# Output projection of the scan: the weights first in the DMA queue, the bias added to x on POOL instead of on PE

## What is computed

```
out = jnp.swapaxes(ys, 0, 1)
out = out * jax.nn.silu(gate)
out = jnp.einsum('bld,ed->ble', out, w_out) + b_out
if ts > 1:
    out = jnp.repeat(out, ts, axis=1)[:, :L]
...
x = _layernorm(x + _L0_attn_ref(...), axis=-1)
```

## Time and profile before

| | before |
|---|---|
| time, median of 3 runs | 3907.22 us (3903.13 to 3920.8) |
| time of the profiled execution | 3888.8 us |
| its span in the trace | 3887.2 us |
| mean granted TensorE clock | 0.91 |
| PE busy | 3273.1 us, 84% of the span |
| DVE busy | 2940.3 us, 76% |
| ACT busy | 2034.9 us, 52% |
| POOL busy | 1158.9 us, 30% |

### The profile page before, as it was taken

How to read it: one execution, slowest core, us unless ns; L and a number is a source line. 1 busy time by engine, 2 the same in 40 slices (tenths; PEclk the granted TensorE clock), 3 DMA queues, 4 the chain that set the end, 5 groups by cost and what they waited for, 6 DMA issues and landing times. The chain is left out here.

```text
span 3887.2 us, 70295 instructions
## 1 busy us (share of the span) xinstructions
PE 3273.1 (84%) x25130; PEld 2242.6 (58%) x25130; DVE 2940.3 (76%) x5069; ACT 2034.9 (52%) x4097; POOL 1158.9 (30%) x1404
## 2 busy tenths in 40 slices
PE   4677777771799957799999999999999955999997
PEld 1677677741688856444444444444444434888886
DVE  7999999841333447588898888988899325888888
ACT  3444444410354433256778878888888832333333
POOL 5888888605311244100111111212111120000000
PEclk7788888875899978688999999999999977999999
DMA  3000000023222126420303031220200000000001
GB/s 137 1 1 0 0 0 0 0 79 123 90 86 86 65 92 191 90 38 8 46 13 46 13 46 27 37 39 21 45 15 13 12 20 13 11 10 12 12 12 44
DMA packets 85787, 155.14 MB, mean 40 GB/s; under 512 B 16688, under 2 KB 53445, under 8 KB 83570
## 3 DMA queue, kind: packets, MB, share of 16 engines
q1 hardware_dynamic: 65202, 108.32, 11.4%
q0 software_dynamic: 19584, 42.14, 3.4%
q10 hardware_dynamic: 768, 1.57, 0.3%
HBM read 92.70 MB, written 59.51 MB: 39 GB/s over the span
## 5 line engine op out<-in xcount | busy, mean ns | idle before, releaser
L1772 DVE TENSOR_REDUCE row_max<-psum 128x2 f32<-128x1024 f32 (+2 forms) x1152 | 1271.2, 1133 | 174.8 <-PE psum L1646 116.9
L1725 ACT ACTIVATE probs_T<-psum 128x512 f32<-128x512 f32 (+3 forms) x2304 | 1154.9, 562 | 314.2 <-PE psum L1670 168.3
L370 PE MATMUL psum<-h_hist,stream 128*128 128x192 f32 x2816 | 500.9, 343 | 230.8 <-ACT h_hist L351 230.8
L1690 PE MATMUL psum<-probs_T,v_all 128*17 128x256 f32 (+1 forms) x8704 | 686.5, 383 | 0.8 <-issue 0.8
L1646 PE MATMUL psum<-k_rows,q_rows 48*128 48x512 f32 (+3 forms) x2304 | 643.2, 465 | 39.5 <-DVE row_max L1772 22.5
L1670 PE MATMUL psum<-q_rows,k_rows 50*128 50x512 f32 (+3 forms) x2304 | 671.6, 430 | 1.7 <-DMA q_rows<-max_parts 1.4
L325 POOL TENSOR_TENSOR x_times_b<-x_slab,B_sb 128x384 f32<-128x384 f32 (+1 forms) x828 | 623.6, 818 | 81.9 <-DVE psum L276 74.0
L370 PEld LDWEIGHTS psum<-h_hist,stream 128*128 128x128 f32 x2816 | 494.5, 203 | 237.7 <-ACT h_hist L351 155.3
L351 ACT ACTIVATE h_hist<-psum 128x384 f32<-128x384 f32 (+1 forms) x828 | 339.5, 453 | 359.4 <-DVE psum L276 359.4
L1670 PEld LDWEIGHTS psum<-q_rows,k_rows 50*128 50x128 f32 x2304 | 327.8, 189 | 249.5 <-ACT probs_T L1725 206.4
L2020 PE MATMUL psum<-x_T,w_part 128*128 128x512 f32 x1632 | 404.4, 397 | 24.9 <-POOL w_part L2080 24.9
(11 more groups left out here) (214 smaller groups left out, 3238.7 us busy)
## 6 DMA issues: line engine op xcount, KB each, us to landing
w_raw<-in_w SPq DMA_DIRECT2D x16, 1024.0 KB, 8.0
qk_rows<-qk_split SPq DMA_DIRECT2D x64, 256.0 KB, 3.3
q_rows<-qk_rows SPq DMA_DIRECT2D x42, 256.0 KB, 11.8
k_rows<-qk_rows SPq DMA_DIRECT2D x42, 256.0 KB, 16.8
inbox<-zeros SPq DMA_DIRECT2D x8, 1024.0 KB, 10.4
xe_sb<-inbox SPq DMA_DIRECT2D x8, 1024.0 KB, 5.9
outbox<-ye_sb POOLq DMA_DIRECT2D x8, 1024.0 KB, 10.2
o_raw<-o_acc POOLq DMA_DIRECT2D x64, 128.0 KB, 2.0
```

The lines of the kernel that those rows point to most:

```text
L370: last = pe.matmul(ps[:, 1 + j, 0:BL * DH * CHUNKS], diag[:, s, :], hist[:, j, :, :, :].rearrange("p t h (s c) -> p (t h) s c", s=NS)[:, : ...
L1690: last = pe.matmul(ps[at:at + HD + 1, 7, lo:HALF], k.v[:, kt, 2 * (n // 4) + j, :], pt[:, u % RING_P, j, HALF * half + lo:HALF * (half + 1 ...
L1725: act.activation(pt[:, u % RING_P, j, o:CH], ps[:, S_BANKS + at_item % RING_ST, o:CH], ACT.Exp, scale=SCALE).then_inc(taken, 1)
L1772: dve.tensor_reduce(mx[:, n % 4, heads[0]:heads[-1] + 1, QT * c + i % QT, mm], ps[:, banks, 0:width], AX.X, ALU.max).then_inc(maxed, 1)
```

## The change

The load of w becomes the first DMA of the stage. b_out is loaded into all 128 partitions instead of one, and second. Then come two pieces of x, wg, and the other six pieces. The one-row product is gone from PE. Instead POOL adds b_out to x in place, one instruction of 1024 elements per partition for each group, after the group's x has landed; DVE's first addition of a group waits for that (`biased`) instead of for x. PE waits at its start for w alone, and for wg only before the first scores.

```
@@ -515,11 +515,11 @@
-        bo = sb("b_out_sb", [1, D])
+        bo = sb("b_out_sb", [P, D])
...
         @block.sync
         def _(sp):
-            for g in range(NG_LN):
+            def load_x(g):
                 rows = slice(g * LNG // 2, (g + 1) * LNG // 2)
                 sp.dma_start(k.stream[:, :, :].rearrange("p (i j) c -> p i (j c)", j=2)[:, rows, :],
                              a["x"].rearrange("(i p j) c -> p i (j c)", p=P, j=2)[:, rows, :]).then_inc(x_in[g], 16)
-                if g == 0:
-                    sp.dma_start(w[:, :, :], a["w_out_T"].rearrange("(h p) e -> p h e", p=P)).then_inc(loaded, 16)
-            sp.dma_start(bo[:, :], a["b_out"].rearrange("(o e) -> o e", o=1)).then_inc(loaded, 16)
+
+            sp.dma_start(w[:, :, :], a["w_out_T"].rearrange("(h p) e -> p h e", p=P)).then_inc(loaded, 16)
+            sp.dma_start(bo[:, :], a["b_out"].partition_broadcast(P)).then_inc(bo_in, 16)
+            load_x(0)
+            load_x(1)
             sp.dma_start(wg[:, :, :], a["wg"].rearrange("(h p) e -> p h e", p=P)).then_inc(wg_in, 16)
+            for g in range(2, NG_LN):
+                load_x(g)
             fold["load"](sp)
 
         @block.gpsimd
         def _(pool):
             fold["zeros"](pool)
+            pool.wait_ge(bo_in, 16)
+            for g in range(NG_LN):
+                pool.wait_ge(x_in[g], 16)
+                tiles = k.stream[:, g * LNG:(g + 1) * LNG, :]
+                pool.tensor_tensor(tiles, tiles, bo[:, :].unsqueeze(1).to_broadcast([P, LNG, D]), ALU.add).then_inc(biased, 1)
...
-                    dve.wait_ge(x_in[i * 2 // LNG], 16)
+                    dve.wait_ge(biased, i * 2 // LNG + 1)
...
             def scores(g):
+                if g == 0:
+                    pe.wait_ge(wg_in, 16)
...
-            pe.wait_ge(loaded, 32)
-            pe.wait_ge(wg_in, 16)
+            pe.wait_ge(loaded, 16)
...
                 for h in range(DH):
-                    pe.matmul(acc, k.gateT[:, h, i * P:(i + 1) * P], w[:, h, :], start=(h == 0), stop=False)
-                pe.matmul(acc, k.ones[0:1, :], bo[:, :], start=False, stop=True).then_inc(projected, 1)
+                    last = pe.matmul(acc, k.gateT[:, h, i * P:(i + 1) * P], w[:, h, :], start=(h == 0), stop=(h == DH - 1))
+                last.then_inc(projected, 1)
```

More of the change, by code:

```diff
@@ L521, in project_out @@
         logits_T = sb("route_logits_T", [E_MOE, T])
-        loaded, wg_in, z_ready, projected, added = (sem("po_" + n) for n in ("loaded", "wg_in", "z", "proj", "added"))
+        loaded, bo_in, biased, wg_in, z_ready, projected, added = (sem("po_" + n) for n in ("loaded", "bo_in", "biased", "wg_in", "z", "proj", "added"))
         x_in = [sem(f"po_x_in{g}") for g in range(NG_LN)]
```

## The result

| | before | after |
|---|---|---|
| median of 12 runs | 3909.37 us (3900.2 to 3925.3) | 3876.8 us (3860.62 to 3896.78) |
| ratio, 95% interval | | 0.9928 [0.9905, 0.9951] |
| profiled execution: time, span | 3888.8, 3887.2 us | 3876.54, 3874.9 us |
| the stage, first DMA to barrier | 78.63 us | 61.61 us |
| mean granted clock | 0.91 | 0.90 |

What follows compares the result with a forecast made beforehand. PE was taken to set the stage's pace, waiting 17.1 us for wg and starting at half clock. Second turn 19.6 us plus one-row products 5.0 gave 24.6 off 3907.2: 3882.6 us, range 3873 to 3899.

Steps and rivals of the forecast that it cites:

- w and PE's start: Stage start: w, now loaded first, lands at 792.0 us, so PE starts there instead of at 803.5.
- The rival of a late w: Stage start: w lands like x's slowest piece, PE starts at 799.2; gain 19.5 us, 3887.7 us; chance 0.06.
- x and b_out: Loads behind w: 393 kB more than before, costing 1.01 us at 389 GB/s, so both are there at 793.7 us.
- POOL's addition: Bias on POOL: 2.3 us per group, first ending at 796.0 us; only that one on the path.
- Line 498 beside POOL: DVE's normalizing tensor_scalar, 407 ns: taken to run at one element a time, unblocked by POOL's additions, costed at nothing.
- The rival built on it: Normalization of group 0: four instructions each wait for a POOL addition, 7 us later; gain 17.6, 3889.6 us; chance 0.12.
- Second turn: PE's turn for group 1, after DVE's first three groups: at 808.3 us instead of 827.89, a gain of 19.6.
- The clock: PE's clock in the stage: rises 3.5 us after PE's start without one-row products, instead of 21.6.
- The cold clock to the end of the stage: Rival: PE's clock never rises in the stage; 4.4 us slower, 3911.6 us; chance 0.05.
- Rounds: Two pairs on PE after the second turn: 4.97 us instead of 6.21; eight one-row products gone save 5.0 us.
- Tail: From the turn of group 5 to the barrier: same instructions, 14.9 us as before.
- The extra gain from warm fold products: After the barrier, 96 small products of 19.98 us take half if the clock stays up: 3872.6 us; chance 0.05.

Runs made afterwards that it cites:

- e1: The changed kernel measured and profiled a second time, nothing altered: stage 61.79 us, ratio 0.9954 against the kernel before.
- e2: Kernel before with only the loads reordered, bias still a one-row product on PE, no POOL addition: stage 67.54 us, ratio 0.9968.
- e3: Kernel before with only the bias moved to POOL, loads in the old order, b_out to all partitions: stage 74.25 us, ratio 0.9971.
- e4: Changed kernel, the stage's normalization made a scalar_tensor_tensor reading 1/std from PSUM: stage 57.20 us, ratio 0.9952 against the kernel before.
- e5: Changed kernel with each POOL addition of 1024 elements cut into four of 256: stage 59.20 us, ratio 0.9923 against the kernel before.
- e9: The kernel of e2 with the bias product on PE over all 128 rows instead of one: stage 59.77 us, one run.
- e10: Changed kernel without POOL's eight additions, so the output lacks this bias; DVE waits for x itself: stage 51.27 us, one run.
- e12: The kernel of e8 with the bias of groups 0 and 1 on PE as full-row products, the rest on POOL: stage 52.90 us, ratio 0.9916.
- e7: Changed kernel with w, b_out and wg loaded two stages earlier into own tiles: stage 59.66 us, ratio 0.9962 against the kernel before.
- e8: Changed kernel with the edits of e4 and e7 together: stage 54.04 us, ratio 0.9911 against the kernel before.
- e11: The kernel of e8 with POOL's addition cut into one of 512 elements per pair: stage 53.72 us, ratio 0.9907 against the kernel before.

## Why the prediction was right, and where it was not

The sign and the range held: 3876.8 us lies in 3873 to 3899, 5.8 from the forecast. The stage did not give the 24.6 us of the sum, though: it gave 17.0, and the forecast came near in whole time because the first measurement's difference (28 us, 19 to 37) was larger than what the stage shows. That is luck: e1, the same kernel, gave 18. By the sum's own terms:

- *w and PE's start:* right, 2.92 us after the first DMA for 3.0. The rival of a late w fell. The loads are the larger part of the gain (e2: 11.1 of 17.0).
- *x and b_out:* "there at 793.7", 4.7 us in. It was 7.27; DVE's first addition came 2.6 us late. I had priced the added bytes at 389 GB/s; the queue moved 126 to 197 from the second to the fifth microsecond and 337 to 368 in the next three. Nor did b2 show the higher rate: its 1 MB in 4.98 us, from issue to use, is some 210 GB/s.
- *POOL's addition:* right, 2.33 us for 2.3, eight without a gap, and DVE waited for POOL once.
- *Line 498 beside POOL, "I cost it at nothing":* this is the step that failed. It cost 8.08 - 1.38 = 6.7 us. I read the mode of the instruction off its duration: 407 ns lies on the line of the additions, so it would go at one element at a time and not block. e3, e4 and e5 show that it blocks all the same. A duration on another operation's line did not tell what the instruction has to wait for. The Trainium skill, page "SBUF — State Buffer", section "Who interferes with whom", has the rule that the second to come waits for the whole of the other's instruction; the trace agrees with it for DVE, 2423 ns beside POOL's 2382, and not for POOL, whose additions grew from 2330 to 2382 and not by 407; the rule, which I had weighed against the row, was right where it mattered. The rival built on it, 17.6 us of gain, was the case that happened; that its number came within 0.6 us owes something to terms that offset each other: x 2.6 us late, the rounds 1.3 and DVE's groups 0.5 better.
- *Second turn:* 28.16 instead of 19.35 us after the first DMA. 8.8 late: 2.6 by x, 6.7 by line 498, less 0.5 for DVE's groups, which took a little less than I had put. The gain there is 38.94 - 28.16 = 10.8 us and not 19.6.
- *The clock:* right, 3.8 us after PE's start for 3.5, and the reason given, that the one-row products are gone, is what e9 bears out. The closeness is partly chance: in the other eleven kernels without them the rise came 2.9 (e4) to 6.1 us (e10) after PE's start. That PE's first pauses would be too short to lose the clock was wrong with line 498 in the way (11.32 us); nor was the 4.6 us read from one fall a safe bound, since in e12 the clock fell 2.3 us after PE's last product. The cold clock to the end of the stage did not come: from 818.03 on the turns take 1.04 to 1.09 us.
- *Rounds:* 4.61 us for 4.97. A one-row product costs (6.21 - 4.61) / 2 = 0.80 us of a round, not 0.62: the product ahead of it is slower too (1.06 us to 0.86, e2 and e9). From the second turn to that of group 5 it is 18.50 us instead of 24.83, 6.3 gained for the 5.0 of the sum.
- *Tail:* 14.95 us for 14.9. The extra gain from warm fold products did not come: they take 20.66 us, against 19.98.

So 10.8 + 6.3 - 0.1 = 17.0 us.

## What to carry to other kernels

Before moving work to POOL beside a busy DVE, list DVE's instructions in that stretch that a trace has shown blocked there (here tensor_scalar, a copy, and operations on two SBUF tensors), and price each at the length of a POOL instruction. Reading and writing SBUF alone is not enough to be blocked: the batch-norm statistics (408 to 430 ns) and the reciprocal (144 ns) ran beside POOL's additions as without. An operand in PSUM took the normalization out of the way for some 70 ns, and shorter POOL instructions shortened the wait. A product with one row is no cheap product: at full clock it took longer than one over 128 rows, and a stage that mixes it in stayed at half clock for over 20 us. Where two engines wait for each other by turns, one late step can cost more than its own time, since the pause can drop PE's clock; take the milestone's lateness from both engines.

## What the runs showed of the hardware that I had not expected

- tensor_scalar with two per-partition scalars, 407 ns for 256 elements alone, takes 2423 ns beside POOL additions of 2382, and 808 beside such of 726. POOL hardly notices: 2382 ns beside it, 2330 at the least. Beside DVE's gate products, both inputs in SBUF, it was POOL that took longer, 3084 and 3017 ns (e7, e8) and, by pairs, 2319 instead of 1273 (e11), while those products kept their 0.69 us. Why the tensor_scalar takes 407 ns alone stays open.
- With one-row products between full ones PE's clock stayed at 0.50 for 21.6 and 22.5 us of unbroken work; without them it rose 2.9 us (e4) to 6.1 us (e10) after PE's start, over twelve traces (3.8 in that of the change, 6.0 in e9).
- It fell in PE's pauses of 2.83 us (e12), 4.91 (e4, e8) and longer, and did not in those of 2.25 (e10) and 2.39 (e4). The fall came 2.3 us (e7, e12) to 4.55 us (after) after PE's last product.
- The load that copies one row to all partitions, standing second in the queue, landed 5.2 to 5.9 us after issue in five runs and 3.6 in one; 128 different rows landed after 3.1. One run of the latter does not settle it.
